# Four buffers for gathered rows, routed results taken at the head of DVE's step, shared down weights scaled early

## The reference

```python
mod = silu(c) @ wmod                    # six rows of 256 per batch: sa, ca, ga, sb, cb, gb
ga, gb = sign * max(abs, 0.25)          # a gate per batch and column
h = layernorm(x) * (1 + ca) + sa
x = x + ga * linear_attention(h)        # 16 heads of 16, blockwise decay, RMS norm, gate u, W_out
h = layernorm(x) * (1 + cb) + sb
x = x + gb * (shared_mlp(h) + sum over the top 2 of 8 experts of weight * expert_mlp(h))
# mlp(h) = (silu(h @ gate.T) * (h @ up.T)) @ down.T, inner width 512
```

## Time and profile before

| | us |
|---|---|
| median of 3 runs (range) | 412.12 (411.83 to 412.14) |
| the profiled execution | 412.94 |
| its span | 411.1 |
| PE / DVE / ACT / POOL busy | 382.4 / 283.0 / 252.1 / 192.7 |

### The profile page before, as it was taken

One profiled execution on the slowest core, in us unless ns is written; L12 is line 12 of the kernel. 1 busy time (PEld: TensorE's weight loads), 2 busy tenths in 40 slices (PEclk: granted clock), 3 DMA queues, 4 the chain that ended last, 5 costly groups with the idle time before them and its releaser, 6 DMA issues.

```text
span 411.1 us, 13319 instructions
## 1 busy us (share of the span) xinstructions
PE 382.4 (93%) x5186; PEld 329.3 (80%) x5186; DVE 283.0 (69%) x560; ACT 252.1 (61%) x541; POOL 192.7 (47%) x192
## 2 busy tenths in 40 slices
PE   7999998999978969799999999989999999999992
PEld 4645556788867759789999999989899989999991
DVE  6886488788789856579886576667667675454542
ACT  4588666666586544648458767676585764554530
POOL 1000005477766875112255465665655765655330
PEclk8799998999999998999999999999999999999998
DMA  8960020000770029990422143343334343342324
GB/s 271 318 88 16 2 103 2 3 15 28 257 244 30 27 64 338 326 324 18 81 71 62 42 66 66 55 67 66 53 57 76 55 65 66 56 77 41 35 34 115
DMA packets 26260, 38.81 MB, mean 94 GB/s; under 512 B 4996, under 2 KB 20340, under 8 KB 26072
## 3 DMA queue, kind: packets, MB, share of 16 engines
q1 hardware_dynamic: 16120, 25.53, 19.5%
q0 software_dynamic: 7488, 10.27, 15.4%
q10 hardware_dynamic: 2592, 2.18, 1.6%
HBM read 27.60 MB, written 10.36 MB: 92 GB/s over the span
## 4 chain that ended last, share of the span: by engine, by line
DMA 39%; PE 22%; DVE 19%; issue 10%; ACT 6%; ACTq 1%; DVEq 1%; POOL 1%; SPq 0%; POOLq 0%
DMA out<-tmp,dk 34%; PE ps L1301 6%; PE ps L1493 5%; DVE wx L924 4%; PE ps L1513 2%; DMA wx<-in_wexp 2%; DVE xres L987 1%; DVE tmp L1001 1%; DVE tmp L1150 1%; DVE st L990 1%; PE ps L1287 1%; DMA tmp<-h2rows,src_i 1%; DMA tmp<-in_decay_tables 1%; DVE rs L1019 1%; ACTq L692 1%
## 5 line engine op out<-in xcount | busy, mean ns | idle before, releaser
L1493 PE MATMUL ps<-tmp,wx 128*128 128x128 bf16 x2640 | 158.0, 220 | 1.5 <-ACT tmp L744 1.5
L1493 PEld LDWEIGHTS ps<-tmp,wx 128*128 (+1 forms) x2640 | 150.5, 98 | 1.7 <-issue 1.7
L525 POOL DMA_INDIRECT out<-tmp,dk x39 | 66.2, 1698 | 62.9 <-DMA out<-tmp,dk 57.4
L753 ACT ACTIVATE tmp<-tmp 128x512 bf16<-128x512 f32 x55 | 34.6, 630 | 75.9 <-PE ps L1513 39.8
L1513 PE MATMUL ps<-wx,tmp 128*128 (+1 forms) x660 | 80.9, 273 | 0.2 <-DVE tmp L1156 0.2
L1513 PEld LDWEIGHTS ps<-wx,tmp 128*128 128x128 bf16 x660 | 62.0, 98 | 7.1 <-DVE tmp L1156 0.5
L1162 DVE SCALAR_TENSOR_TENSOR woutg<-modr,w_hl,woutg 128x256 f32<-128x256 f32 x39 | 19.1, 491 | 56.9 <-ACT woutg L762 56.9
L518 POOL DMA_INDIRECT tmp<-h2rows,src_i x39 | 41.3, 1059 | 20.5 <-issue 10.2
L1150 DVE TENSOR_TENSOR tmp<-ps,tmp 128x512 f32<-128x512 f32 x55 | 37.9, 688 | 14.3 <-PE ps L1493 7.2
L1156 DVE TENSOR_TENSOR tmp<-tmp 128x512 bf16<-128x512 f32 x55 | 38.2, 694 | 7.3 <-ACT tmp L753 7.2
L924 DVE TENSOR_TENSOR wx<-ps,wx 128x2048 f32<-128x2048 f32 x16 | 36.4, 2275 | 1.3 <-PE ps L1321 1.3
(11 more groups left out here) (186 smaller groups left out, 597.6 us busy)
## 6 DMA issues: line engine op xcount, KB each, us to landing
wx<-in_wexp SPq DMA_DIRECT2D x27, 512.0 KB, 5.5
xres<-in_x SPq DMA_DIRECT2D x4, 512.0 KB, 7.0
h2rows<-h2s ACTq DMA_DIRECT2D x16, 128.0 KB, 3.4
out<-h2s SPq DMA_DIRECT2D x12, 128.0 KB
h2s<-in_wmod SPq DMA_DIRECT2D x1, 1024.0 KB, 9.5
wx<-decay_rows SPq DMA_DIRECT2D x16, 64.0 KB
modr<-mod_rows SPq DMA_DIRECT2D x1, 1024.0 KB, 4.7
wx<-in_wqkvu SPq DMA_DIRECT2D x1, 768.0 KB, 7.2
```

What stands on the lines that cost most here:

```text
L525: e.indirect_dma_start(t["out"], bass.IndirectOffsetOnAxis(ap=dst_i[:, j:j + 1], axis=0), yb[(NA + j) % 2], None, compute_op=ALU.add).then ...
L753: e.activation(hs[p][:, 0:FF], hf[p], ACT.Copy).then_inc(s["inner_high"], 1)
L1493: ins = e.matmul(half(bank, m * P), weight(at_, weights(part, w) + k * FF + m * P, P), xT[p][:, (2 * a + k) * P:(2 * a + k + 1) * P], star ...
```

## The change

Three edits. Gathered rows get four buffers instead of two, so that gather k waits for tile k-4 instead of k-2; GpSimd's order stays gather k behind scatter k-7. On DVE `take_result(f-3)` moves from the end of the step to its head, and the gate is made by DVE alone as gate0 + batch * (gate1 - gate0), the difference being made once by GpSimd. The shared down weights are loaded at about the time of the projections into parts of `h2s` that are not yet in use, scaled by GpSimd at n = 0 to 3, and the four splits are at steps 2, 9, 11 and 13, the two down parts first.

```diff
+NXG = 4
+PARTS_AT, SCALED_AT = (2, 9, 11, 13), (0, 1, 2, 3)
@@ SP
+            e.wait_ge(s["mod_products"], 2)
+            for a in range(2):
+                e.dma_start(raw_down[a], t["wexp"][NSH, :, 2, a * PIECE // 2:(a + 1) * PIECE // 2]).then_inc(s["down_loaded"], 16)
...
-            for q in range(NPIECE):
+            for q in range(2):
                 e.dma_start(early_stage[:, q * PIECE:(q + 1) * PIECE], t["wexp"][NSH, :, q, :]).then_inc(s["shared_loaded"], 16)
...
-            e.wait_ge(s["shared_low"], NPIECE + 1)
+            e.wait_ge(s["shared_low"], len(SHARED_PARTS))
@@ GpSimd
-                if 14 <= n < 18:
-                    scale_down((n - 14) // 2, n % 2)
+                if n in SCALED_AT:
+                    scale_down(SCALED_AT.index(n) // 2, SCALED_AT.index(n) % 2)
+            e.wait_ge(s["second_scaled"], 2)
+            e.tensor_tensor(modr[:, 1, 3], modr[:, 1, 3], modr[:, 0, 3], ALU.subtract).then_inc(s["gate_difference"], 1)
             def gather(j):
-                wait(e, "weight_made", j - 1)
+                wait(e, "weight_made", j - NXG + 1)
...
+            gather(2)
+            gather(3)
+            add_x1(NA - 4)
+            add_x1(NA - 3)
+            for j in range(NXG, NG + NXG):
+                if j < NG:
+                    gather(j)
+                if j - NXG < 2:
+                    add_x1(NA - 2 + j - NXG)
...
+                if j >= NXG + 2:
+                    add_rows(j - NXG - 2)
+            add_rows(NG - 2)
+            add_rows(NG - 1)
@@ ScalarE
+                    if h == NT - 8:
+                        e.wait_ge(s["shared_low"], 1)
+                    if h == NT - 4:
+                        e.wait_ge(s["shared_low"], 2)
...
-                weigh_gate(f - 2)
@@ DVE
-            def scale_gate(f):
+            def make_gate(f):
                 if is_tile(f) and routed(f):
                     j = f - NA
-                    wait(e, "gate_weighted", j + 1)
-                    e.scalar_tensor_tensor(out=gates[f % 2], in0=modr[:, 1, 3], scalar=batch[:, j:j + 1], in1=gates[f % 2],
+                    wait(e, "result_made", j - 1)
+                    if j == 0:
+                        e.wait_ge(s["gate_difference"], 1)
+                    e.scalar_tensor_tensor(out=gates[f % 2], in0=modr[:, 1, 3], scalar=batch[:, j:j + 1], in1=modr[:, 0, 3],
...
             for f in range(f, NF + 3):
+                take_result(f - 3)
                 inner_low(f - 1)
                 make_inner(f)
-                scale_gate(f - 2)
-                take_result(f - 3)
+                make_gate(f - 2)
@@ TensorE
-                if f < B:
-                    e.wait_ge(s["shared_low"], NPIECE + f)
...
-                    e.wait_ge(s["shared_low"], 2)
+                    e.wait_ge(s["shared_low"], len(SHARED_PARTS))
                     e.wait_ge(s["state_made"], NSTATE)
                     turn_rows(0)
```

More of the change, by code:

```diff
@@ L180, in home @@
             return wx[:, at_:at_ + 2 * PIECE].bitcast(f32)
-        early_stage = att[:, 0:NPIECE * PIECE]
+        early_stage = att[:, 0:2 * PIECE]
+        raw_down, first_down = ([early_rows[:, (c + NC * b) * D:(c + 2 + NC * b) * D] for b in range(2)] for c in (NC - 2, NC - 4))
         rt = w_parts[:]
@@ L205, in build @@
         slots_i, first = (route(TOP * NT, i32) for _ in range(2))
-        dest, empty, low_part, batch, other = (route(NG) for _ in range(5))
-        late_i = route(NG, i32)
+        dest, empty, low_part, batch = (route(NG) for _ in range(4))
         of_slots = dk[:].rearrange("p h d -> p (h d)")
@@ L543, in _ @@
             add_x1(NA - 5)
-            for j in range(NG + 4):
-                if j + 2 < NG:
-                    gather(j + 2)
-                if j < 4:
-                    add_x1(NA - 4 + j)
-                if j == 4:
+            gather(2)
[7 more added lines that the diff above has]
+                    add_x1(NA - 2 + j - NXG)
+                if j == NXG + 2:
                     e.wait_ge(s["rows_found"], 2)
@@ L753, in middle @@
                     e.activation(hs[p][:, 0:FF], hf[p], ACT.Copy).then_inc(s["inner_high"], 1)
-            def weigh_gate(f):
-                if is_tile(f) and routed(f):
-                    j = f - NA
-                    wait(e, "result_made", j - 1)
-                    if j == 0:
-                        e.wait_ge(s["ranks"], 2)
-                        e.wait_ge(s["routing"], RT_FLAGS)
-                    e.activation(gates[f % 2], modr[:, 0, 3], ACT.Copy, scale=other[:, j:j + 1]).then_inc(s["gate_weighted"], 1)
             def softmax():
@@ L1024, in step_attention @@
                     e.wait_ge(s["shared_high"], x + 1)
+                    if x < 2:
+                        low, high = (a_.rearrange("p (b n) -> p b n", b=B) for a_ in (low, high))
                     e.tensor_tensor(low, whole_, high, ALU.subtract).then_inc(s["shared_low"], 1)
@@ L1169, in take_result @@
                     wait(e, "rows_added", 16 * (j - 1))
-                    wait(e, "gate_scaled", j + 1)
+                    wait(e, "gate_made", j + 1)
                     wait(e, "weight_made", j + 1)
@@ L1434, in turn_rows @@
                     j = f - NA
[L1435 to L1436 removed]
+                    e.wait_ge(s_xg[j % NXG], 16 * (j // NXG + 1))
+                    rows = xg[j % NXG][:, 0:D].bitcast(bf16)
                 else:
```

66 lines of the change are left out of this document (34 added, 32 removed).

## The result

The changed kernel took 395.79 us (median of 4 runs, 394.02 to 396.76) against 411.98 for the kernel before on the same chip (409.61 to 412.14): ratio 0.9628, 95% interval 0.9586 to 0.9669, so 16 us faster. That is more than the 403.1 forecast and outside the range (398.5 to 408.5). It went the way of the first rival, TensorE as the bound, and beyond its 399.6.

The account below looks back on a forecast made before the run. The serial chain of scatter-adds was taken to bound the kernel, with TensorE close behind. From 412.12 us, 6.6 us on the scatters and 2.4 us upstream came off, 9.0 in all, giving 403.1 us; range 398.5 to 408.5.

Parts of the forecast that it names:

- the first rival: Routed stage: TensorE becomes the bound if scatters shorten too; 399.6 us with 4 us upstream; chance 0.18.
- the four buffers: Gathers of routed rows: costed at nothing, since each gather stands behind the same scatter in GpSimd's queue as before.
- the head wait: DVE's step: result m waits for scatter m-2 to land; bites after 30 tiles by under 1 us, costing nothing.
- The first scatter: Start of routed results: about 7 us earlier than 234.07, from 4.7 plus 2.4.
- Nothing in the change shortens a scatter: Routed stage: the argument against TensorE becoming the bound, which needed 0.2 us less over 26 scatters.
- the third rival: Routed stage: scatters grow longer where DVE's split and gate run beside them; up to 412.6 or 416 us; chance 0.08.
- The chain's interval: Routed scatters: 4.36 us each before, 4.31 after (163.9 over 38), against TensorE's 4.21; scatters still set the end.
- my 6.6: Saving on the scatters: 4.7 us from an earlier first scatter plus 1.9 us from results ready ahead of their scatters.
- 3.5 us to spare: Tail before the change: TensorE ended at about 403.4, the sums were reloaded 3.5 us later.
- The cost of nothing for the gate: Gate on ScalarE and DVE: moving it to DVE alone counted nothing, neither engine being the bound beside TensorE's 4.21 us.
- Upstream: Early down weights, ahead of the routed tiles: net -2.4 us, from -3.8 and +1.4, with ends of +1 and -5.
- +1.4: Attention loop: time lost because the weight splits stand apart, at steps 9, 11 and 13, plus one at step 2.

Follow-up runs that it names:

- head_two: Kernel before with result at the head of DVE's step, DVE's gate and GpSimd's new order; two buffers, late down weights: 405.48 us, ratio 0.9849.
- two_buffers: Changed kernel with two buffers of gathered rows instead of four, GpSimd's new order kept: 396.83 us, ratio 0.96.
- plain_copies: Kernel before with DVE's subtractions for the expert weights' low halves made one-input copies, low values left out: 409.67 us, ratio 0.9947.
- gate_alone: Kernel before with only the gate made by DVE alone; result still last, weights late, two buffers: 406.66 us, ratio 0.9849.
- late_result: Changed kernel with the result taken at the end of DVE's step again, DVE's gate kept: 401.14 us, ratio 0.9697.
- head_only: Kernel before with only the result at the head of DVE's step and DVE's gate; two buffers, late down weights: 404.0 us, ratio 0.9749.
- kept_busy: Kernel before with 40 extra small matmuls on TensorE in its idle stretch before 154 us: 413.51 us, ratio 1.0033.

## Why the prediction was wrong

The sign and the order of things held: scatters set the end before, the four buffers give nothing by themselves in the finished kernel, and the head wait cost TensorE nothing. The first scatter came 12 us earlier, where I had about 7. The sum was 9.0 and the measured gain 16 (17.2 in the spans). Three steps failed, each with its number.

**"Nothing in the change shortens a scatter" was false, and it kept TensorE's bound at 0.18.** The 14 profiles hold 546 scatters. 95 of them started while one of DVE's operations on two SBUF inputs, a split or a low half, was running and had over 0.17 us left. All 95 grew, to 1.64 to 2.37 us on GpSimd, and the length of each is what that operation had left plus 1.46 us, within 0.04. The other 451 took 1.55 to 1.63 us, but for six of head_two (1.64 to 1.80) that started beside DVE's gate operation, which has two SBUF inputs as well. How long the two run side by side does not count: in 93 of the 451 such an operation began behind the scatter's start and ran 0.6 us or more beside it. A pair of each kind, from the kernel before (the split ends at 296.44, and 0.33 + 1.46 = 1.79) and from two_buffers:

```profile
295.23 1.21 DVE L936 TENSOR_TENSOR wx<-wx  x1
...
296.11 1.79 POOL L525 DMA_INDIRECT out<-tmp,dk  x1 [1.22 <-DMA out<-tmp,dk]
```

```profile
227.53 1.59 POOL L542 DMA_INDIRECT out<-tmp,dk  x1 [0.72 <-DMA out<-tmp,dk]
...
228.00 1.22 DVE L960 TENSOR_TENSOR wx<-wx  x1
```

Of the 39 scatters 17 were held like this in the kernel before (4.4 us in all), 4 in plain_copies and none in the changed one. I had this in the third rival, with the wrong sign: I reasoned that a scatter passes through all phases of DVE's step. It does not while it is tied to its result. Before, the result is followed at once by the split and the low half, and the scatter, 0.8 us behind, starts while one of them runs. Taken at the head, the result is followed by one low half, and then DVE stands for TensorE; the changed kernel's rows show where the two-input work went:

```profile
297.88 1.59 POOL L542 DMA_INDIRECT out<-tmp,dk  x1 [1.47 <-DMA out<-tmp,dk]
...
298.67 0.69 DVE L1175 TENSOR_TENSOR tmp<-ps,tmp 128x512 f32<-128x512 f32 x1 [1.00 <-PE ps L1520]
299.28 0.47 DVE L1189 SCALAR_TENSOR_TENSOR woutg<-modr,w_hl 128x256 f32<-128x256 f32 x1
...
299.67 1.22 DVE L960 TENSOR_TENSOR wx<-wx  x1
299.77 1.99 POOL L535 DMA_INDIRECT tmp<-h2rows,src_i  x1 [0.30 <-issue]
```

It is the gather that grows now (1.99 us instead of 0.99), and nothing waits for the gather. An operation with a PSUM input holds up no scatter: 119 started while DVE made an inner product (L1175) or a result, each from PSUM, and took 1.55 to 1.63 us. The Trainium skill (SBUF — State Buffer, "Who interferes with whom") holds that a DVE instruction with two SBUF inputs contends with a GpSimd one that reads SBUF, and that the order in which they start decides which of them waits. The trace agrees, by the 95 and the 93. The same section infers that a `tensor_tensor` leaves the writing of descriptors alone; the splits and low halves are such operations and held these indirect transfers by up to 0.78 us (2.37 instead of 1.59), so here the measurement decides.

**The chain's interval was taken as the chain's own.** I moved it from 4.36 to 4.31 and let it end the kernel. It was made of three things: scatters tied to late results, by ScalarE's gate (gate_alone: -5.9 us) and by the place (late_result: 3 to 5 us behind the changed kernel); scatters lengthened by DVE (plain_copies: -2.2); and late landings, of which each costs 1.2 us or more when the chain is the bound. These prices overlap and are not a sum. Free of the first two it runs at 4.1 us (the median interval of head_only is 4.13), faster than TensorE's 4.21, and follows. Hence the -10.6 us behind the turn of tile 0 instead of my 6.6: 5.2 in TensorE's waits for rows, 5.0 in the tail behind TensorE's end, the rest before the turn at 219.73. The tail also put the rival's own number off: I gave TensorE 3.5 us to spare, the wait for the reload, and left out that two of the four additions and their stores come forward with it (5.0 instead of 3.5). With 6.7 instead of 4 us upstream that covers its distance from the measured time. The cost of nothing for the gate is part of this step: I looked at the engines' load, and the gate was a wait on the path.

**Upstream was mis-sized: -6.7 instead of -2.4.** In the attention loop itself I expected +1.4. The last product of the profiled pair stands 0.06 us later, and from the fourth product on, where the profiles agree, the loop takes 67.9 us instead of 67.6; but the first product stands at 57.51 before and 56.82 after, and one interval near 70 us is 5.05 in some profiles and 6.4 in others of the same code, so this term is not measured better than by 1.5 us. Behind the loop I allowed 3.8 and got 6.7, in which all kernels with early weights agree. By the rows, the first turn came 3.2 us earlier against the last product (11.19 to 7.99), not 2.75: the wait is not all there is to win, for the matmuls ahead of it waited for the same held operations. To the matmul of the 1.52 us wait another 2.6 (12.96 to 10.39), of which 0.84 can be the clock's, by kept_busy, that I had counted at 0; from there to the ranks' matmul 0.9 (180.32 to 173.72, where the 0.72 us wait is gone too). I had credited the fourth split with 1.04 and stopped counting there.

What would have caught it: the 60.7 and 67.4 us could not be known, but the phase could. The earlier trace rows gave 1587, 1787 and 2151 ns for one and the same operation, and asking what DVE was doing as each of the short and the long ones started answers the first step and points at the second.

## What to carry to other kernels

Where one operation's time spreads over a range on an engine with nothing else to do, line up its instances with what other engines are running when each one starts before taking the mean for its cost; reordering the neighbour can be the cheapest cure. A serial chain and an engine of nearly the same rate hide each other: work out both ends, with their own tails, for after the change, and do not let a chain whose cause you remove keep its old interval. Cost an off-path operation by who waits for its result, not by how busy its engine is.

## What the runs showed of the hardware

- GpSimd's part of a scatter-add of 128 rows from SBUF took 1.55 to 1.63 us undisturbed. Started while a DVE operation on two SBUF inputs ran, it took what that operation had left plus 1.46 us (95 cases, up to 2.37 us). Such an operation that began later did not lengthen it. A gather of 128 rows took 0.97 to 1.0 us undisturbed for the most part and up to 2.0 held up.
- A scatter whose result has just been made starts about 0.80 us behind it and never less than 0.76, against 0.27 us behind the landing before it.
- Nearly two thirds of the chained scatters start 4.0 to 4.25 us behind the last one; now and then one comes 5.2 to 6.0 us behind. In the seven profiles that record each landing, eleven landed 3.3 to 4.1 us behind the end of GpSimd's part, where 2.2 us is the median. They stand at varying places, and no run tells the cause.
- 40 small matmuls in an idle stretch kept the granted clock at 1.00 where it had been 0.67 over the 5 us behind; the 13 us stretch there was 0.84 us shorter.
- What lies ahead of the expert stage varies by up to 2.4 us from run to run of the same code: the last attention product stood between 141.0 and 143.4 us in the seven profiles with late weights.
